# Three TensorE semaphores of the graph attention given by a drain instead of by the last matmul

## The reference, cut to what matters

```python
Qh = (x @ Wq.T + bq).reshape(n, H, D)
Kh = (x @ Wk.T + bk).reshape(n, H, D)
Vh = (x @ Wv.T + bv).reshape(n, H, D)
Ee = (edge_attr @ We.T + be).reshape(-1, H, D)
score = (Kh[src] * Qh[dst] * (1.0 / np.sqrt(D)) * Ee).sum(-1)
score = jnp.exp(jnp.clip(score, -5.0, 5.0))
msg = Vh[src] * score[..., None]
wV = jax.ops.segment_sum(msg, dst, num_segments=n)
```

## Time and profile before

| | us |
|---|---|
| Median of three runs | 14131.57 (14116.25 to 14145.13) |
| Span of the profiled execution | 13943.9 |
| Median less the span | 187.7 |
| The attention's gathers, first start to last end (busy and idle time of their group) | 5460.3 |
| PE busy, whole span | 7881.3 (57%) |
| POOL busy, whole span | 7746.7 (56%) |
| DVE busy, whole span | 5002.0 (36%) |
| ACT busy, whole span | 2112.3 (15%) |

### The profile page before, as it was taken

The page is one execution under the profiler, slowest core; times in us unless marked ns, Lnnn a source line. Parts: engine busy times, 40 slices in busy tenths (PEclk is TensorE's granted clock), DMA queues, the critical chain, the costliest instruction groups (busy, mean ns, idle before and its releaser), DMA issues.

```text
span 13943.9 us, 198796 instructions
## 1 busy us (share of the span) xinstructions
PE 7881.3 (57%) x55262; PEld 6966.0 (50%) x55263; DVE 5002.0 (36%) x11869; ACT 2112.3 (15%) x4676; POOL 7746.7 (56%) x8220
## 2 busy tenths in 40 slices
PE   4566656565665556556655565445555555555554
PEld 4555545555554444455545454444444444444454
DVE  3333333333333233333333334333333334333334
ACT  1111111111111000000000012222222222222222
POOL 5555655555555555655555556555555555555554
PEclk7766766766676666666666675555555555555555
DMA  3222222222222111121111112222222222222221
GB/s 62 55 50 52 54 54 50 51 50 49 50 48 49 41 44 42 42 45 42 40 43 40 39 43 65 61 59 59 59 58 57 57 56 56 56 55 53 54 53 51
DMA packets 861613, 712.24 MB, mean 51 GB/s; under 512 B 474896, under 2 KB 730544, under 8 KB 860544
## 3 DMA queue, kind: packets, MB, share of 16 engines
q0 software_dynamic: 260000, 369.16, 12.3%
q1 hardware_dynamic: 515345, 225.59, 6.8%
q10 hardware_dynamic: 85325, 105.63, 2.2%
HBM read 584.55 MB, written 115.24 MB: 50 GB/s over the span
## 4 chain that ended last, share of the span: by engine, by line
another core or an unknown queue 41%; PE 25%; issue 18%; DVE 8%; DVEq 4%; ACT 3%; ACTq 1%; POOL 0%; DMA 0%; POOLq 0%; SPq 0%
PE ps_kv L727 4%; PE ps_kv L718 3%; PE ps_e L704 3%; PE ps_sum L889 2%; PE ps_sum L687 2%; PE ps_q L687 2%; PE ps_hot L687 2%; ACT node_q L1014 1%; PE ps_t L696 1%; DVE score L1484 1%; DVE ps_t L1481 1%; PE ps_kv L736 1%; DVE attention_space L1482 1%; DVEq L420 1%
## 5 line engine op out<-in xcount | busy, mean ns | idle before, releaser
L591 POOL DMA_INDIRECT kv<-kv_rows,src_ids x3125 | 2948.0, 943 | 2512.3 <-DVE message L1490 1659.0
L591 POOL DMA_INDIRECT kv<-in_x,src_ids x2500 | 2358.9, 944 | 1805.8 <-issue 924.5
L591 POOL DMA_INDIRECT kv<-h_rows,src_ids x2500 | 2360.9, 944 | 1761.2 <-issue 917.3
L889 PE MATMUL ps_sum<-message,node_h 128*128 128x64 f32 x6260 | 1475.2, 422 | 272.3 <-DVE message L1490 259.1
L889 PEld LDWEIGHTS ps_sum<-message,node_h 128*128 128x128 f32 x6260 | 1402.7, 332 | 304.5 <-DVE message L1490 285.4
L718 PE MATMUL ps_kv<-between,hot 128*128 128x490 bf16 x2500 | 883.4, 500 | 975.2 <-ACT node_q L1014 618.3
L687 PE MATMUL ps_sum<-kv,hot 128*128 128x65 f32 x5000 | 940.6, 355 | 262.3 <-issue 219.3
L687 PEld LDWEIGHTS ps_sum<-kv,hot 128*128 128x128 f32 x5000 | 924.4, 277 | 286.7 <-issue 286.1
L687 PE MATMUL ps_hot<-kv 128*128 128x65 f32 x1880 | 412.7, 396 | 1041.6 <-issue 900.3
L687 PEld LDWEIGHTS ps_hot<-kv 128*128 128x128 f32 x1880 | 385.2, 306 | 1115.1 <-issue 1113.1
L718 PEld LDWEIGHTS ps_kv<-between,hot 128*128 128x128 bf16 x2500 | 289.5, 129 | 1293.6 <-issue 995.4
(11 more groups left out here) (242 smaller groups left out, 11227.5 us busy)
## 6 DMA issues: line engine op xcount, KB each, us to landing
node_q<-in_edge_attr SPq DMA_DIRECT2D x125, 480.0 KB
edge_space<-ee_rows SPq DMA_DIRECT2D x125, 480.0 KB
kv<-kv_rows,src_ids POOLq DMA_INDIRECT x3125
kv<-in_x,src_ids POOLq DMA_INDIRECT x2500
node_q<-in_edge_attr SPq DMA_DIRECT2D x125, 320.0 KB
kv<-h_rows,src_ids POOLq DMA_INDIRECT x2500
edge_space<-ee_rows SPq DMA_DIRECT2D x125, 320.0 KB
ee_rows<-node_q ACTq DMA_DIRECT2D x25, 1440.0 KB
```

The lines of the kernel that those rows point to most:

```text
L591: nc.gpsimd.indirect_dma_start(out=into_slot, out_offset=None, in_=table_rows, in_offset=bass.IndirectOffsetOnAxis(ap=ids, axis=0),).then_ ...
L889: mm = nc.tensor.matmul(to, one_hots[:, k, :], messages[:, k, :], start=(k == 0), stop=(k == K - 1))
```

## The change

Three places in the attention's TensorE stream give their semaphore by a drain instruction behind the last transpose or matmul and no longer by that transpose or matmul. `sum_messages` also serves the extra rounds, so their `x.summed` changes as well. `x.hot_t` and `x.query` of the extra rounds and every semaphore of the two summing passes are given as before. All data operations, their operands and their order are the same.

```diff
@@ turn_hots
                 for k in range(K):
-                    tp = nc.tensor.transpose(ps_hot[:, k * P:(k + 1) * P], hot[:, u, k, :], ident16[:])
-                tp.then_inc(p.hot_t, 1)
+                    nc.tensor.transpose(ps_hot[:, k * P:(k + 1) * P], hot[:, u, k, :], ident16[:])
+                nc.tensor.drain().then_inc(p.hot_t, 1)
@@ sum_messages
                 for k in range(K):
-                    mm = nc.tensor.matmul(to, one_hots[:, k, :], messages[:, k, :], start=(k == 0), stop=(k == K - 1))
-                mm.then_inc(done, 1)
+                    nc.tensor.matmul(to, one_hots[:, k, :], messages[:, k, :], start=(k == 0), stop=(k == K - 1))
+                nc.tensor.drain().then_inc(done, 1)
@@ extra_queries
-                nc.tensor.matmul(ps_query[u][:, 0:1], ones16[:], zeros16[:, 0:1], start=False, stop=True).then_inc(p.query, 1)
+                nc.tensor.matmul(ps_query[u][:, 0:1], ones16[:], zeros16[:, 0:1], start=False, stop=True)
+                nc.tensor.drain().then_inc(p.query, 1)
```

## The result

The changed kernel takes 14762.97 us (median, 14748.47 to 14820.99) beside 14133.35 us for the kernel before (14116.25 to 14145.13): 1.0454 times as long, 95% interval 1.0432 to 1.0476. It is slower, by some 630 us, where 1240 us of gain were forecast. The time also lies above the range.

The account below looks back on a forecast made before the run. Late TensorE semaphores inside runs of gathers were taken to bound the attention. On-time drains give -1557 us, extra rounds +320 us, together -1240 us: 14131.6 us falls to 12892 us, range 12570 to 14500 us.

Parts of the forecast that it names:

- What bounds the kernel: Attention: TensorE semaphores falling into runs of gathers come 4 to 15 us late; groups take 8.74 us, POOL's pace 6.23.
- A drain gives it from the sequencer: Drains inside gathers: semaphore on time, 0.05 us behind the work, as the trace's one PE drain; chance 0.58.
- -1557 us: Attention's gathers: POOL no longer waits 1659 us for messages, but 102 us of gaps between gathers remain.
- PSUM's acknowledgement is the late part: Matmul semaphores: PSUM's acknowledgement of all bytes could be late, and a drain would wait for it, holding PE.
- Price of a drain: Three drains a group on PE: 0.27 us each (0.05 to 0.45), chain from 3.60 to 4.4 us a group.
- POOL's pace hides it: Attention: the chain with drains, 4.4 us a group, stays below POOL's 6.23 us, which hides the drains' price.
- 0.8 x 625 = 500 us: Attention: what the drains would cost over 625 groups without the cover of POOL's pace.
- Extra rounds, +320 us: Attention's 97 extra rounds: behind group 300 the chain exceeds POOL's pace, 325 groups losing 1.0 us each.
- 12.3 us: Time one extra round adds to a plain group's chain: 5.7 us without gathers plus 5.0 and 1.6 us of waits.
- The span and the median: Whole kernel: the median lies 187.7 us above the profile's span, and the same is kept for the changed kernel.
- a drain that stands as long as the semaphore was late: Slower rival, attention: held drains delay sums and queries, 2.4 to 4 us over 312 stretches, +750 to +1250 us; chance 0.20.
- The signs: Changed profile: "another core" share under 20%, remote waits gone, POOL's message idle some 400 us, drain medians below 0.7, some 2.5.

Follow-up runs that it names:

- the bare drains: Kernel before with matmuls still giving the semaphores and three drains without any behind them: 1.0263 and 1.026 on 10.44 ms chips, 1.042 on a 13.91 ms chip.

## Why the prediction was wrong

**What bounds the kernel.** Right in its place: TensorE's semaphores come late inside runs of gathers. The two experiments without indexed gathers take 2310 and 2324 us off (POOL's pace of 6.23 us went with the lateness there, so this is not the lateness alone). It read one thing too much into the earlier trace rows: that PE works on while a semaphore is pending doesn't show that a drain behind that work would end.

**"A drain gives it from the sequencer, as the one in the trace did 0.05 us behind the work. I take that value."** This is the step that failed, and with it the -1557 us. The row it was taken from the earlier trace rows is a drain with no gather beside it, and of such drains the value holds: in the run without gathers none ends more than 0.05 us behind the matmul before it. Inside gathers they stand up to 18.7 us. The prediction wrote down that no row shows this, and then took the near value with 0.58. The Trainium skill's sentence in "PSUM — Partial Sum Buffer", "Engine vs sequencer instructions", that a drain waits for the engine to go fully idle, is what the trace shows here (6.43 us for work over after 0.8). That PSUM's acknowledgement is the late part, as the prediction worked out from two pages of the Trainium skill, fits, but no run separates it from other things for which a drain may wait.

**Price of a drain.** The second failed step, a mis-sized term: 0.27 us taken, 0.45 us as upper end, 0.52 to 0.53 us measured (0.50 us where drains give no semaphore). A group's chain went from 3.60 to 5.15 us, not 4.4 (3.75 to 4.95). The estimate added the drain's end, a branch and a load; the starts above show what it left out, that the next instruction started before the last one's end at all three places, by 0.13 to 0.21 us, and now it starts 0.22 to 0.54 us behind that end.

**POOL's pace hides it.** Right as a sum, 6.23 us predicted and 6.25 us measured where POOL is the bound. But that cover exists only if the lateness is gone. It was not, so the drains cost 0.9 to 1.0 us a group. The prediction's own sentence for the lost cover, 0.8 x 625 = 500 us, is near the 560 to 630 us measured, but by luck in part: its drain was too cheap by half, and part of the true price is free under the lateness.

**Extra rounds, +320 us.** Not tested: POOL never became the bound of the changed kernel. `x.hot_t` kept its wait (ACT's copy of the extra rounds waits 497 us by `remote`, 484 before). The shape that was forecast, POOL as the bound in the first half and the extra rounds in the second, is what the bare drains show on a chip of 10.44 ms. Their 324 us behind messages are no proof of the term's size, though: no semaphore is late there, and lateness made up 6.6 of its 12.3 us.

**The span and the median.** The 187.7 us between them were carried over as a constant. They are none of the kernel's: in each later run the profiled execution's time is 1.8 us above its span. So the profile of before is of an execution of some 13946 us, and the median is of executions of 14116 to 14145 us. The record doesn't say on which chips; 13946 us is near the chips of 13.9 ms, so the spans of before and after (+809 us) probably mix two chips. Against the change's trace from a chip of 13.91 ms the gathers' stretch grew by 2947.9 + 3067.1 - 5460.3 = 555 us, near the 560 us of that run.

```profile
L591 POOL DMA_INDIRECT kv<-kv_rows,src_ids x3125 | 2947.9, 943 | 3067.1 <-DVE message L1491 2235.2 <-issue 830.6 <-DVE node_h L1477 1.4
```

**The rivals.** The one that came true is the first, a drain that stands as long as the semaphore was late. Its size was too large, 750 to 1250 us against 630: it let each of 312 held stretches grow by 2.4 to 4 us; the one above is 0.8 us longer than that of the earlier trace rows, and the long intervals grew by 1.16 us in the mean and became fewer. What it named as the cost, the holding, is mostly free; what costs is, by the counts, mainly the drains' bare price in the short stretches. Its decision point, drains more than 1 us beyond the work, was passed by 332 drains. It was given 0.20.

**The signs.** Most of the forecast's signs came true with the forecast wrong: the share of "another core" fell to 7.9%, the `remote` waits of L1063 and L1497 vanished, the drains' medians were 0.695 and 2.363 us, and the stages before kept their time within 0.8%. They only say that a wait got a recorded releaser. What told was POOL's idle time behind messages, 1659 us, expected near 400, found at 2405, and the drains' longest.

No version that does the whole work was found to beat both kernels. Those that lose the lateness do so by not gathering.

## What to carry to other kernels

Moving a semaphore from an instruction to a drain changed who reports and not when: where completions were late, the drain was late too and held the engine's queue. Price a drain where the engine's instructions overlap by the lost start-ahead and the restart, some 0.5 us here (by the counts that made up more of the loss than the holding), and look for its cover in the kernel as it will be if the hoped-for gain fails. Judge such a change by the idle time of the engine that should become the bound and by the longest drains, and not by a median or by the name in the chain of waits.

## What the runs showed of the hardware

- The same kernel takes 10.44 ms on two chips and 13.88 to 14.13 ms on the others, with the same clock level in the attention (0.50) and the same gathers (0.943 us each). In none of the six traces from the first two is a wait ended by `remote`, and the stages before the attention end at some 6480 us and not at 8420; on the others the waits of the earlier trace rows are there. The kernel before itself has a trace only from a slower one. A profile from one chip can't be summed with a median from another.
- What makes completions late is the gather by index on GpSimd: 128 such rows of 128 bytes do it as 128 rows of 512 bytes do (1.0001), while as many plain DMAs of rows at fixed places, by SyncE or by GpSimd, don't (0.8336, 0.8331). Whether it is the indexing or the scattered rows isn't shown. How these gathers hold TensorE's completions, and why on some chips only, stays open.
- A drain on TensorE costs some 0.5 us between overlapping matmuls, with a semaphore on it (0.52 us in the quiet group) or without (0.50 us). Where completions were late, drains stood for up to 18.7 us in the changed kernel; without gathers, and on the chips of 10.44 ms, none ended more than 0.1 us behind the matmul before it.
